# Reordering VectorE's first work in a routed-expert and gated-MLP kernel, and ending the block without GpSimd's drain

## The chip, the cores and the metric

The kernel runs on one core of a Trainium2 chip. Five engines work side by side, each with an instruction stream of its own: TensorE (PE in the views; its weight loads are PEld), VectorE (DVE), ScalarE (ACT), GpSimd (POOL) and SyncE (SP), which only starts transfers. They wait for each other through semaphores. The metric is device microseconds of one execution; fewer is better.

## What is computed

Tokens are normed, sent through one of four "experts" chosen by token id (all three products of an expert use the same 512x512 matrix from `ctx_2048`), added back under a gate, normed again and sent through a gated MLP of inner width 1408:

```python
def _L0_xattn_ref(hidden_states, token_ids, Wg, Wu, Wd):
    expert_ids = jnp.minimum(jnp.clip(token_ids, 0, VOCAB - 1) // (VOCAB // 4), 3)
    for e in range(4):
        g = jax.nn.silu(jnp.einsum('bsd,fd->bsf', hidden_states, Wg[e]))
        u = jnp.einsum('bsd,fd->bsf', hidden_states, Wu[e])
        y = jnp.einsum('bsf,df->bsd', g * u, Wd[e])
        out = jnp.where((expert_ids == e)[..., None], y, out)
    return out

x = x + jnp.tanh(g_xattn[0]) * _L0_xattn_ref(_layernorm(x), ids, ctx, ctx, ctx)
x = x + jnp.tanh(g_ffn[0])   * _L0_ffn_ref(_layernorm(x), gate_w, up_w, down_w, gate_s, up_s, down_s)
# ffn: silu(x @ gate_w.T * gate_s) * (x @ up_w.T * up_s) @ down_w.T * down_s
```

There are 2048 tokens of width 512, all float32. This is a reading cut of the reference: clipping, reshapes and the excluded inputs are left out.

## The kernel before

**Stages.** First a routing stage sorts the 2048 tokens by expert into 19 tiles of 128 slots (16 tiles of tokens and up to 3 more, since every expert's tokens are padded to whole tiles). It is a chain of small VectorE operations and of matmuls with one-hot matrices. From it come: `gidx`, which rows of `x` GpSimd gathers for each tile (column 0 is made first, by a product of its own, so that tile 0 can be fetched early; columns 1 to 18 follow at L620); `sidx`, where GpSimd stores a finished tile; `tiles` and from it `packed`, which expert each tile has, which TensorE reads into registers (L996); and a second set of one-hots, `is_low`, `is_high` and `in_tile` (L636 to L642), for a product (L991) that gives `oidx`, the order in which results are written at the very end.

Then come 19 expert steps, one for each tile, then the MLP in four blocks of four tiles, each block with 11 chunks of the inner width. The last four tiles' results are scaled, added and stored one by one.

**Products in two parts.** Every float32 operand is held as a high part (rounded, ScalarE: `ctx_hi`, `x_hi`, `h_hi`) and a low part (the rest, VectorE: `ctx_lo`, `x_lo`, `h_lo`). An expert product (`expert_product`, L951) is 12 matmuls in three passes of four: high by high, low `x` by high weights, high `x` by low weights. Its third pass waits for the low parts of the expert's matrix, `ctx_lo` of 4 chunks each, 16 chunks for the four experts (`ctx_lo(n_from, n_to)`, L740).

**A tile's way.** GpSimd gathers its rows; VectorE takes `stats` (L648 to L653), GpSimd the inverse deviation (`inverse_std`, L375), VectorE applies it (`norm`, L659); TensorE transposes (`turn_x`, L948), ScalarE and VectorE split (`x_hi` L464, `x_lo` L686); TensorE makes the first product (L962), ScalarE the silu (L472), VectorE the product with it (`hidden`, L697); TensorE transposes that (`turn_h`, L977), it is split (`h_hi` L468, `h_lo` L701), and the second product's result is added by VectorE (`update`, L708) and stored by GpSimd (L369).

**Order.** Every engine's order is written out by hand. TensorE's in the expert stage is `first_product(k)`, `turn_x(k+1)`, `second_product(k-1)`, `turn_h(k)`. VectorE's `step(k)` holds its share of it, and the 16 `ctx_lo` chunks are laid between the first steps by hand (L747 to L768). ScalarE's first work is `ctx_hi(0)`, `ctx_hi(1)`, `x_hi(0)`, `ctx_hi(2)`, `silu(0)`, `x_hi(1)`, `ctx_hi(3)`, the gates' tanh, and then `h_hi(0)`. SyncE loads experts 0 and 1, then waits for tile 0's rows before it loads experts 2 and 3 (L247 to L249). GpSimd's order is gather 0, 1 and 2, then `inverse_std(0)` and `inverse_std(1)`, then gather 3.

While experts run, the MLP's weights `raw` (L262) are loaded in 16 pieces and split, and rows of the down weights are loaded once more as `checked` (L272) to see whether they have low bits at all (`check`, L719). They have two slots, `c % 2`.

## Time and profile before

| | |
|---|---|
| median of 3 runs | 405.64 us (405.2 to 405.85) |
| the profiled execution's own time | 406.21 us |
| its span, from the first instruction to the last | 404.4 us |
| PE busy | 375.8 us, 93% of the span |
| DVE busy | 239.6 us, 59% |
| ACT busy | 139.8 us, 35% |
| POOL busy | 91.3 us, 23% |

The profile describes one execution, so its times of instructions belong to the 406.21 us one. The 1.8 us between that and its span lie before the first or behind the last instruction. Busy shares are averages over stages that have different limits; the order of time within the first 46 us and the last 6 us is what matters here.

### The profile page before, as it was taken

The page shows a single profiled execution, that of the slowest core. Times are in us where ns is not written, and L with a number is a line of the kernel's source. Part 1 is how long each engine was busy: PE and PEld are TensorE (multiplying, and loading weights), DVE is VectorE, ACT ScalarE, POOL GpSimd, SP SyncE. Part 2 cuts the span into 40 slices and gives each one's busy share as a digit, 9 for nine tenths or more (in the row PEclk, how much of TensorE's full clock was granted, in tenths as well). Part 3 has the DMA queues.
Part 4 walks back from the last instruction along what each step waited for, and adds up shares of the span by engine and source line. Part 5 has one row for each costly group of instructions (what it writes and reads, how often), then busy time and mean ns, then how long its engine had stood idle before and what let it go on. Part 6 is the DMA issues. An engine that isn't in the chain of part 4 may idle for free.

```text
span 404.4 us, 6054 instructions
## 1 busy us (share of the span) xinstructions
PE 375.8 (93%) x1775; PEld 307.6 (76%) x1775; DVE 239.6 (59%) x457; ACT 139.8 (35%) x241; POOL 91.3 (23%) x132
## 2 busy tenths in 40 slices
PE   3299999999999879999999999999999999999991
PEld 2267788888888667788888888888888888888880
DVE  6879878888888875635537225636325646322244
ACT  3264454555454334623232222322222231222220
POOL 6335545454542121001102101101201001200003
PEclk9999999999999999999999999999999999999996
DMA  6757444455625324420000220000220000100002
GB/s 208 258 162 220 134 140 149 142 173 181 210 84 158 122 74 150 118 105 0 0 2 26 79 104 0 0 0 26 78 104 0 0 0 26 76 2 0 0 2 106
DMA packets 14959, 34.55 MB, mean 85 GB/s; under 512 B 2401, under 2 KB 2401, under 8 KB 14945
## 3 DMA queue, kind: packets, MB, share of 16 engines
q1 hardware_dynamic: 10624, 20.21, 15.7%
q0 software_dynamic: 4320, 14.16, 10.2%
q8 instruction: 8, 0.13, 0.1%
q14 instruction: 7, 0.05, 0.0%
HBM read 25.19 MB, written 9.18 MB: 85 GB/s over the span
## 4 chain that ended last, share of the span: by engine, by line
PE 83%; DVE 7%; DMA 3%; issue 2%; POOL 2%; ACT 1%; POOLq 0%; DVEq 0%; SPq 0%; ACTq 0%
PE bank L1059 37%; PE bank L962 22%; PE bank L1066 18%; PE bank L948 4%; DMA rows<-dwT 2%; PE bank L977 2%; DVE work L744 1%; DMA x_rows<-rows,sidx 1%; POOL minus_j L346 1%; DVE xn L659 1%; DVE work L701 1%; DVE work L686 0%; DVE rows L708 0%; ACT work L460 0%; DVE rows L860 0%
## 5 line engine op out<-in xcount | busy, mean ns | idle before, releaser
L1059 PE MATMUL bank<-work,wgu 128*128 (+1 forms) x720 | 167.3, 385 | 1.5 <-DVE work L686 1.3
L1059 PEld LDWEIGHTS bank<-work,wgu 128*128 128x128 f32 x720 | 133.0, 188 | 29.2 <-issue 1.6
L962 PE MATMUL bank<-work 128*128 (+1 forms) x432 | 111.4, 407 | 1.6 <-ACT work L464 0.7
L962 PEld LDWEIGHTS bank<-work 128*128 128x128 f32 x432 | 80.1, 192 | 19.1 <-issue 1.9
L1066 PE MATMUL bank<-work,hp 128*128 128x512 f32 x352 | 88.5, 394 | 0.5 <-DVE hp L831 0.5
L826 DVE SCALAR_TENSOR_TENSOR sh<-bank,gs,sh 128x512 f32<-128x512 f32 (+1 forms) x45 | 33.2, 738 | 88.1 <-PE bank L1059 88.0
L1066 PEld LDWEIGHTS bank<-work,hp 128*128 128x128 f32 x352 | 65.1, 188 | 13.9 <-DVE hp L831 0.9
L521 ACT ACTIVATE sh<-bank,gs 128x512 f32<-128x512 f32 (+1 forms) x45 | 30.5, 678 | 86.3 <-PE bank L1059 85.5
L525 ACT ACTIVATE hp<-sh 128x512 fp32r<-128x512 f32 (+1 forms) x45 | 28.0, 622 | 84.5 <-DVE sh L826 84.5
L375 POOL TENSOR_TENSOR rstd<-ve,half 128x1 f32<-128x1 f32 x31 | 19.7, 635 | 131.4 <-DVE ve L653 131.2
L831 DVE TENSOR_TENSOR hp<-sh,hp 128x512 fp32r<-128x512 f32 (+1 forms) x45 | 30.6, 681 | 30.2 <-ACT hp L525 30.0
L447 POOL DMA_INDIRECT out<-rows,oidx x16 | 16.1, 1008 | 116.9 <-DVE rows L860 94.2
L686 DVE TENSOR_TENSOR work<-bank,work 128x512 fp32r<-128x512 f32 (+1 forms) x35 | 23.9, 684 | 1.5 <-ACT work L464 0.9
L464 ACT ACTIVATE work<-bank 128x512 fp32r<-128x512 f32 (+1 forms) x35 | 20.5, 590 | 12.4 <-PE bank L948 8.6
L948 PE MATMUL bank<-ident,xn 128*128 128x128 f32 x124 | 19.6, 283 | 4.5 <-DVE xn L659 4.5
L948 PEld LDWEIGHTS bank<-ident,xn 128*128 128x128 f32 x124 | 15.6, 145 | 9.6 <-DVE xn L659 6.1
L659 DVE TENSOR_SCALAR xn<-rows,mv,rstd 128x512 f32 (+1 forms) x31 | 17.0, 550 | 9.0 <-POOL rstd L375 9.0
L472 ACT ACTIVATE sh<-bank 128x512 f32<-128x512 f32 x19 | 11.4, 598 | 28.5 <-PE bank L962 28.4
L648 DVE BATCH_NORM_STATS2 bn<-rows 128x6 f32 (+1 forms) x31 | 21.2, 684 | 0.0
L708 DVE SCALAR_TENSOR_TENSOR rows<-bank,tg,rows 128x512 f32 (+1 forms) x19 | 14.2, 749 | 7.3 <-PE bank L962 7.3
L715 DVE TENSOR_TENSOR wgu<-raw,wgu (+1 forms) x16 | 14.3, 892 | 6.3 <-issue 6.3
L482 ACT ACTIVATE junk<-wgu 128x704 f32 x16 | 12.7, 794 | 13.2 <-DVE wgu L715 13.2
(126 smaller groups left out, 235.6 us busy)
## 6 DMA issues: line engine op xcount, KB each, us to landing
raw<-guT SPq DMA_DIRECT2D x16, 352.0 KB
ctx_in<-ctxT SPq DMA_DIRECT2D x4, 1024.0 KB, 7.9
rows<-x_rows SPq DMA_DIRECT2D x8, 512.0 KB, 4.1
checked<-dwT SPq DMA_DIRECT2D x11, 256.0 KB, 3.4
rows<-dwT SPq DMA_DIRECT2D x11, 256.0 KB, 3.0
dsb<-down_s SPq DMA_DIRECT2D x1, 256.0 KB, 8.1
out<-rows,oidx POOLq DMA_INDIRECT x16, 2.7
rows<-x,inow POOLq DMA_INDIRECT x12, 4.0
```

The lines of the kernel that those rows point to most:

```text
L464: act.activation(xpart(b, u, 0), turned[:, :], ACT.Copy).then_inc(S["xhi_ready"], 1)
L521: act.activation(sh[:, part], gate_ps(i)[:, part], ACT.Silu, scale=gs[:, 0, c:c + 1])\
L525: act.activation(hslot(c)[:, 0, part], sh[:, part], ACT.Copy)\
L648: dve.bn_stats(bn[:, 0, :], rows[:, ds(at, 1), :]).then_inc(S["bn_parts"], 1)
L659: dve.tensor_scalar(xn[:, :], rows[:, ds(at, 1), :], mv[:, 0, 0:1], rstd[:, 0:1], ALU.subtract, ALU.mult).then_inc(S["xn_ready"], 1)
L686: dve.tensor_tensor(xpart(b, u, 1), turned[:, :], xpart(b, u, 0).bitcast(F32), ALU.subtract)\
L826: dve.scalar_tensor_tensor(out=sh[:, part], in0=up_ps(i)[:, part], scalar=gs[:, 1, c:c + 1], in1=sh[:, part], op0=ALU.mult, op1=ALU.mult). ...
L831: dve.tensor_tensor(hslot(c)[:, 1, part], sh[:, part], hslot(c)[:, 0, part].bitcast(F32), ALU.subtract)\
L948: mm = pe.transpose(xt_ps[:, c * P:(c + 1) * P], xn[:, c * P:(c + 1) * P], ident[:, :])
L962: mm = pe.matmul(out_ps[:, :], part(s)[:, c * P:(c + 1) * P], ctx_w(e, c, w), start=n == 0, stop=n == last)
L1059: mm = pe.matmul(out_ps[:, tiles.start * P:tiles.stop * P], wgu[:, row + h, w, c * P:(c + 1) * P], moving, start=n == 0, stop=n == last)
L1066: mm = pe.matmul(acc_ps[u][:, :], hslot(c)[:, s, u * P:(u + 1) * P], down_w(c, w), start=c == 0 and n == 0, stop=c == IC - 1 and n == len( ...
```

## The change

VectorE's first work is put in another order. The arithmetic of the second one-hots moves ahead of the copy of `gidx` as far as its small operands go, and the one-hots come right behind that copy. The tables for storing (`sidx`) and for TensorE's registers (`packed`) become a function, `index_tables`, that is called after `norm(0)`. `stats(0)` comes before every `ctx_lo`; all later groups of `ctx_lo` hold one chunk fewer at each point, so that the last group, `ctx_lo(12, 16)`, has four chunks instead of three. TensorE reads its registers from `packed` behind `turn_x(1)` instead of ahead of `turn_x(0)`. SyncE loads a `checked` row when the row two before it is done (it has two slots), instead of the row one before. And the block ends without GpSimd's drain; in its place is nothing, and the other four engines' drain and report become two instructions each.

```diff
--- before.py
+++ after.py
@@ -237,7 +237,7 @@
 
             eng.sem_inc(S["held"])
 
-        block = ctx.enter_context(nc.Block())
+        block = ctx.enter_context(nc.Block(no_gpsimd_drain=True))
 
         @block.sync
         def _(sp):
@@ -291,7 +291,7 @@
                 next_piece(q)
                 before_q = CHECK_AT + RAWS - 2
                 c, c_before, c_checked = (sp.snap(q - before_q), sp.snap(16 * (q - before_q)),
-                                          sp.snap(q - before_q))
+                                          sp.snap(q - before_q - 1))
                 sp.wait_ge(S["check_landed"], c_before)
                 hold(sp)
                 sp.wait_ge(S["bits_done"], c_checked)
@@ -299,7 +299,7 @@
                 check_row(c)
             for c in range(2 + PIECES - checks_from, IC):
                 sp.wait_ge(S["check_landed"], 16 * c)
-                sp.wait_ge(S["bits_done"], c)
+                sp.wait_ge(S["bits_done"], c - 1)
                 check_row(c)
             def load_rows(b):
                 for half_, landed in enumerate((S["rows_a"], S["rows_b"])):
@@ -615,33 +615,36 @@
             dve.scalar_tensor_tensor(out=owner[:, 2, :], in0=tile_at[:, :], scalar=pad_end[0:1, 2:3],
                                      in1=owner[:, 1, :], op0=ALU.is_ge, op1=ALU.add)
             then(dve.tensor_scalar(owner[:, 3, :], tile_at[:, :], pad_end[0:1, 3:4], None, ALU.is_ge))
+            def over_out(a):
+                return a[:, :].unsqueeze(1).to_broadcast([P, TILES, CT])
+
+            then(dve.tensor_scalar(tile_up[:, :], rank[:, :], -(P - 1) / 2, ROUND, ALU.add, ALU.add))
+            dve.scalar_tensor_tensor(out=minus_low[:, :], in0=tile_up[:, :], scalar=ROUND,
+                                     in1=rank[:, :], op0=ALU.subtract, op1=ALU.subtract)
+            then(dve.tensor_scalar(high[:, :], tile_up[:, :], -ROUND, None, ALU.add))
             of_slot = bank[5][:, 0:2 * STEPS]
             dve.wait_ge(S["route_pe"], 4)
             dve.tensor_copy(gidx[:, 1:STEPS], of_slot[:, 1:STEPS]).then_inc(S["tables_ready"], 1)
-            dve.tensor_copy(tiles[:, :, :], owner[:, 2:4, :])
-            then(dve.scalar_tensor_tensor(out=empty[:, :], in0=of_slot[:, STEPS:], scalar=0.0,
-                                          in1=dump[:, :], op0=ALU.is_equal, op1=ALU.mult))
-            for i in range(2):
-                dve.tensor_tensor(shifted[:, i, :], tiles[:, 0, 1 - i:1 - i + PACKED], shifts[:, :],
-                                  ALU.logical_shift_left)
-            dve.scalar_tensor_tensor(out=sidx[:, :], in0=empty[:, :], scalar=-1.0, in1=of_slot[:, STEPS:],
-                                     op0=ALU.add, op1=ALU.add).then_inc(S["tables_ready"], 1)
-            then(dve.tensor_scalar(tile_up[:, :], rank[:, :], -(P - 1) / 2, ROUND, ALU.add, ALU.add))
-            dve.tensor_reduce(packed[:, :], shifted[:, :, :], AX, ALU.bitwise_xor)\
-               .then_inc(S["tables_ready"], 1)
-
-            then(dve.scalar_tensor_tensor(out=minus_low[:, :], in0=tile_up[:, :], scalar=ROUND,
-                                          in1=rank[:, :], op0=ALU.subtract, op1=ALU.subtract))
-            dve.tensor_scalar(high[:, :], tile_up[:, :], -ROUND, None, ALU.add)
+            is_out = is_high[:, 0:TILES, :]
             dve.tensor_tensor(is_low[:, :, :], minus_low[:, :].unsqueeze(1).to_broadcast([P, P, CT]),
                               minus_j[:, :, :], ALU.is_equal).then_inc(S["low_ready"], 1)
-            dve.wait_ge(S["low_ready"], 3)
-            is_out = is_high[:, 0:TILES, :]
-            then(dve.tensor_tensor(is_out, high[:, :].unsqueeze(1).to_broadcast([P, TILES, CT]),
-                                   tile_of[:, 0:TILES, :], ALU.is_equal))
-            dve.tensor_tensor(in_tile[:, 0, 0:TILES, :], is_out,
-                              token[:, :].unsqueeze(1).to_broadcast([P, TILES, CT]), ALU.mult)\
+            then(dve.tensor_tensor(is_out, over_out(high), tile_of[:, 0:TILES, :], ALU.is_equal))
+            dve.tensor_copy(tiles[:, :, :], owner[:, 2:4, :])
+            dve.tensor_tensor(in_tile[:, 0, 0:TILES, :], is_out, over_out(token), ALU.mult)\
                .then_inc(S["route_sb"], 1)
+
+            def index_tables():
+                dve.wait_ge(S["route_sb"], 4)
+                for i in range(2):
+                    dve.tensor_tensor(shifted[:, i, :], tiles[:, 0, 1 - i:1 - i + PACKED], shifts[:, :],
+                                      ALU.logical_shift_left)
+                then(dve.scalar_tensor_tensor(out=empty[:, :], in0=of_slot[:, STEPS:], scalar=0.0,
+                                              in1=dump[:, :], op0=ALU.is_equal, op1=ALU.mult))
+                dve.scalar_tensor_tensor(out=sidx[:, :], in0=empty[:, :], scalar=-1.0,
+                                         in1=of_slot[:, STEPS:], op0=ALU.add, op1=ALU.add)\
+                   .then_inc(S["tables_ready"], 1)
+                dve.tensor_reduce(packed[:, :], shifted[:, :, :], AX, ALU.bitwise_xor)\
+                   .then_inc(S["tables_ready"], 1)
 
             def stats(m, at):
 
@@ -744,28 +747,29 @@
                     dve.tensor_tensor(ctx_w(e, c, 1), ctx_in[:, e, c, :], ctx_w(e, c, 0).bitcast(F32),
                                       ALU.subtract).then_inc(S["ctx_lo"], 1)
 
-            ctx_lo(0, 3)
             landed(0)
             stats(0, ring_slot(0))
+            ctx_lo(0, 1)
+            norm(0, ring_slot(0))
+            index_tables()
+            ctx_lo(1, 3)
+            x_lo(0, 0, 0)
             ctx_lo(3, 4)
-            norm(0, ring_slot(0))
-            ctx_lo(4, 6)
-            x_lo(0, 0, 0)
             landed(1)
             stats(1, ring_slot(1))
-            ctx_lo(6, 7)
+            ctx_lo(4, 5)
             norm(1, ring_slot(1))
-            ctx_lo(7, 9)
+            ctx_lo(5, 8)
             hidden(0)
             x_lo(1, 0, 0)
             landed(2)
             stats(2, ring_slot(2))
-            ctx_lo(9, 10)
+            ctx_lo(8, 9)
             dve.wait_ge(S["gates_ready"], 1)
             step(1)
-            ctx_lo(10, 13)
+            ctx_lo(9, 12)
             step(2)
-            ctx_lo(13, 16)
+            ctx_lo(12, 16)
             with dve.Fori(3, CHECK_AT) as k:
                 step(k)
             dve.wait_ge(S["bits_clear"], 1)
@@ -991,13 +995,13 @@
                 mm = pe.matmul(bank[4][:, 0:TILES], is_low[:, :, c], in_tile[:, 0, 0:TILES, c],
                                start=c == 0, stop=c == CT - 1)
             mm.then_inc(S["route_pe"], 1)
-            pe.wait_ge(S["tables_ready"], 3)
-
-            these, ones_before = [pe.value_load(packed[0:1, i:i + 1], min_val=0, max_val=4 ** PACKED - 1)
-                                  for i in range(2)]
             turn_x(0)
             first_product(0, 0, ctx_ready=KC)
             turn_x(1)
+            pe.wait_ge(S["tables_ready"], 3)
+
+            these, ones_before = [pe.value_load(packed[0:1, i:i + 1], min_val=0, max_val=4 ** PACKED - 1)
+                                  for i in range(2)]
             turn_h(0)
 
             def expert_step(k, e=None, e_before=None, ctx_ready=None):
```

VectorE (DVE), from behind the copy of `gidx` (L620) to the statistics of tile 0, before. `is_low`, `is_high` and `in_tile` are the second one-hots, `empty`, `sidx`, `shifted` and `packed` the tables, `work<-ctx_in` is `ctx_lo`, BN_STATS opens `stats(0)`, `xn` is `norm(0)`:

```order
L622 SCALAR_TENSOR_TENSOR empty<-bank,dump 128x19
L625 TENSOR_TENSOR shifted<-tiles,shifts 1x15 x2
L627 SCALAR_TENSOR_TENSOR sidx<-empty,bank 128x19
L629 TENSOR_SCALAR tile_up<-rank 128x16
L630 TENSOR_REDUCE packed<-shifted 1x2
L633 SCALAR_TENSOR_TENSOR minus_low<-tile_up,rank 128x16
L635 TENSOR_SCALAR high<-tile_up 128x16
L636 TENSOR_TENSOR is_low<-minus_low,minus_j 128x2048
L640 TENSOR_TENSOR is_high<-high,tile_of 128x256
L642 TENSOR_TENSOR in_tile<-is_high,token 128x256
L744 TENSOR_TENSOR work<-ctx_in,work 128x512 x3
L648 BN_STATS bn<-rows 128x6
```

The same engine from behind the same copy (now L627), in the changed kernel:

```order
L629 TENSOR_TENSOR is_low<-minus_low,minus_j 128x2048
L631 TENSOR_TENSOR is_high<-high,tile_of 128x256
L632 CAST tiles<-owner 1x38
L633 TENSOR_TENSOR in_tile<-is_high,token 128x256
L651 BN_STATS bn<-rows 128x6
L654 BN_AGGR mv<-bn 128x2
L656 TENSOR_SCALAR ve<-mv 128x1
L747 TENSOR_TENSOR work<-ctx_in,work 128x512
L662 TENSOR_SCALAR xn<-rows,mv,rstd 128x512
L639 TENSOR_TENSOR shifted<-tiles,shifts 1x15 x2
L641 SCALAR_TENSOR_TENSOR empty<-bank,dump 128x19
L643 SCALAR_TENSOR_TENSOR sidx<-empty,bank 128x19
```

The table rows moved from ahead of the one-hots to behind `xn`; three `work<-ctx_in` no longer stand ahead of BN_STATS; `tile_up`, `minus_low` and `high` moved to before the copy of `gidx`, above the first row shown.

VectorE again, from the MLP piece of step 2 to the loop over the later tiles, before; `wgu` is the piece's low part, `sh` is `hidden(2)`, `rows` is `update(1)`, and `work<-ctx_in` is `ctx_lo` once more:

```order
L715 TENSOR_TENSOR wgu<-raw,wgu 128x704
L697 TENSOR_TENSOR sh<-bank,sh 128x512
L686 TENSOR_TENSOR work<-bank,work 128x512
L708 SCALAR_TENSOR_TENSOR rows<-bank,tg,rows 128x512
L744 TENSOR_TENSOR work<-ctx_in,work 128x512 x3
L769 UNCONDITIONAL_BRANCH
L701 TENSOR_TENSOR work<-bank,work 128x512
```

And in the changed kernel:

```order
L718 TENSOR_TENSOR wgu<-raw,wgu 128x704
L700 TENSOR_TENSOR sh<-bank,sh 128x512
L689 TENSOR_TENSOR work<-bank,work 128x512
L711 SCALAR_TENSOR_TENSOR rows<-bank,tg,rows 128x512
L747 TENSOR_TENSOR work<-ctx_in,work 128x512 x4
L773 UNCONDITIONAL_BRANCH
L704 TENSOR_TENSOR work<-bank,work 128x512
```

One more chunk stands between the update of tile 1 and the low part of tile 2's hidden values, which opens the loop (L701).

TensorE (PE) around the registers, before, from the last products of the routing to the first turn of hidden values (L977):

```order
L929 MATMUL bank<-in_tile,is_low 128x38 x16
L991 MATMUL bank<-in_tile,is_low 128x16 x16
L996 TENSOR_LOAD packed
L996 ISA x2
L996 TENSOR_LOAD packed
L996 ISA x2
L948 MATMUL bank<-ident,xn 128x128 x4
L962 MATMUL bank<-work 128x512 x12
L948 MATMUL bank<-ident,xn 128x128 x4
L977 MATMUL bank<-ident,sh 128x128 x4
```

And in the changed kernel:

```order
L933 MATMUL bank<-in_tile,is_low 128x38 x16
L995 MATMUL bank<-in_tile,is_low 128x16 x16
L952 MATMUL bank<-ident,xn 128x128 x4
L966 MATMUL bank<-work 128x512 x12
L952 MATMUL bank<-ident,xn 128x128 x4
L1003 TENSOR_LOAD packed
L1003 ISA x2
L1003 TENSOR_LOAD packed
L1003 ISA x2
L981 MATMUL bank<-ident,sh 128x128 x4
```

The two loads, with two register instructions each, moved past the first turn, the first product and the second turn.

## Rows read from the trace of the kernel before

**Rows 1.** The page: its span, and the chain that ended last, by engine.

```profile
span 404.4 us, 6054 instructions
...
PE 83%; DVE 7%; DMA 3%; issue 2%; POOL 2%; ACT 1%; POOLq 0%; DVEq 0%; SPq 0%; ACTq 0%
```

**Rows 2.** Windows: stretch, its us, busy us of each engine, PEclk, DMA share, GB/s.

```profile
19.77:25.26 5.49, 5.49 (x13) 4.23 (x14) 4.01 (x8) 2.19 (x4) 1.93 (x2) 1.00 0.68 225
...
45.66:126.17 80.51, 80.51 (x401) 66.29 (x400) 66.60 (x124) 40.53 (x76) 40.04 (x59) 1.00 0.48 150
...
163.75:392.25 228.50, 227.99 (x1043) 189.15 (x1043) 103.47 (x176) 63.42 (x102) 18.93 (x24) 1.00 0.09 31
```

**Rows 3.** Timeline, end of routing: start us, us, engine, line, what [idle before <-releaser].

```profile
9.40 0.22 DVE L617 TENSOR_SCALAR owner<-tile_at,pad_end 1x19 f32<-1x19 f32 x1
...
10.25 0.18 DVE L620 CAST gidx<-bank 128x18 uint32<-128x18 f32 x1 [0.64 <-PE bank L929]
...
10.71 0.94 POOL L364 DMA_INDIRECT rows<-x,gidx  x1 [0.37 <-DVE gidx L620]
...
11.48 1.22 DVE L636 TENSOR_TENSOR is_low<-minus_low,minus_j 128x2048 f16<-128x2048 f16 x1
11.96 1.56 POOL L364 DMA_INDIRECT rows<-x,gidx  x1 [0.30 <-issue]
...
12.81 0.99 SPq L249 DMA_DIRECT2D ctx_in<-ctxT  x2
13.06 0.29 DVE L642 TENSOR_TENSOR in_tile<-is_high,token 128x256 f16<-128x256 f16 x1
13.27 1.89 DVE L744 TENSOR_TENSOR work<-ctx_in,work 128x512 fp32r<-128x512 f32 x3
```

**Rows 4.** Timeline, tile 0's way to the first product, and expert 2's arrival.

```profile
15.08 0.69 DVE L648 BATCH_NORM_STATS2 bn<-rows 128x6 f32<-128x512 f32 x1
...
16.37 0.96 POOL L375 TENSOR_TENSOR rstd<-ve,half 128x1 f32<-128x1 f32 x1 [2.85 <-DVE ve L653]
...
17.37 0.55 DVE L659 TENSOR_SCALAR xn<-rows,mv,rstd 128x512 f32<-128x512 f32 x1 [0.48 <-POOL rstd L375]
...
17.97 1.12 PE L948 MATMUL bank<-ident,xn 128*128 128x128 f32 x4 [3.32 <-DVE xn L659]
...
19.77 5.49 PE L962 MATMUL bank<-work 128*128 128x512 f32 x12 [0.69 <-ACT work L464]
...
20.44 2.19 ACT L460 ACTIVATE work<-ctx_in 128x512 fp32r<-128x512 f32 x4 [0.72 <-DMA ctx_in<-ctxT]
...
25.93 0.69 DVE L697 TENSOR_TENSOR sh<-bank,sh 128x512 f32<-128x512 f32 x1 [1.51 <-ACT sh L472]
...
26.58 2.18 ACT L460 ACTIVATE work<-ctx_in 128x512 fp32r<-128x512 f32 x4
```

**Rows 5.** Line L249, the loads of experts 2 and 3: time from issue to landing.

```profile
DMA to landing us min/median/max: 7.6/8.7/9.8
```

**Rows 6.** Timeline, the last groups of low parts and the products waiting for them.

```profile
34.78 1.89 DVE L744 TENSOR_TENSOR work<-ctx_in,work 128x512 fp32r<-128x512 f32 x3
...
36.20 0.76 PEld L962 LDWEIGHTS bank<-work 128*128 128x128 f32 x4 [0.27 <-issue]
...
37.78 0.66 PE L948 MATMUL bank<-ident,xn 128*128 128x128 f32 x4 [0.38 <-DVE xn L659]
```

**Rows 7.** Timeline, the same for the product of tile 3.

```profile
42.00 1.89 DVE L744 TENSOR_TENSOR work<-ctx_in,work 128x512 fp32r<-128x512 f32 x3
...
44.03 1.17 PE L962 MATMUL bank<-work 128*128 x4 [0.44 <-DVE work L744]
```

**Rows 8.** Line L996: engine, op, count, duration ns min/median/max, first and last start.

```profile
L996 PEldq TENSOR_LOAD <-packed x2: 314/407/500, 13.6 to 14.4; - x2
```

**Rows 9.** Line L76, the barrier at the block's end, columns as above.

```profile
L76 POOLq DRAIN  x1: 5687/5687/5687, 398.5 to 398.5; - x1
...
L76 SPq DRAIN  x1: 7/7/7, 401.7 to 401.7; - x1
```

6 lines of the change are left out of this document (3 added, 3 removed).

## The prediction

> **What bounds the kernel now.** I first read the page's chain by engine and the windows by stage [rows 1, 2]. The reader is to see that PE holds 83% of the chain, and that it is busy for all of the 80.51 us of the steady expert steps and 227.99 of 228.50 us of the MLP. Nothing that VectorE, SyncE or GpSimd do sooner in those stages shows in the end time; they just begin sooner or later as a whole. Time can be won ahead of 45.66 us, where PE still waits, and behind 392 us, where it is done.
>
> Then the timeline of the start [rows 3, 4]. The first product starts at 19.77 at the end of one chain: `in_tile` 13.06, three `ctx_lo` 13.27, statistics 15.08, GpSimd's power 16.37, `xn` 17.37, turn 17.97, `x_hi`, product. PE sat idle 3.32 us for `xn`. But tile 0's rows had landed by 12.81: SyncE starts the loads of experts 2 and 3 when it sees them, and that row starts there. So the statistics stood 2.27 us behind their data, held up by one-hots and weights on their own engine.
>
> Last, the barrier [rows 9]. SyncE, which has seen all results land, drains at 401.7 in 7 ns. GpSimd's drain starts at 398.46 and takes 5.687 us, to 404.15. The span ends at 404.4, so the last 2.4 us are GpSimd's drain alone, although the chain of the page gives it less.
>
> **The change, part by part.**
>
> *Second one-hots sooner.* `tile_up`, `minus_low` and `high` go into the 0.64 us in which VectorE idles ahead of the `gidx` copy at 10.25 [rows 3]. From the last `owner` (9.40, 0.22 long) a dependent step each 0.26 us (estimate from the spacing there) puts the copy at 10.27: no loss. `is_low` then starts at about 10.37 instead of 11.48. From its start to that of `in_tile` were 1.58 us and 0.29 of `in_tile`, so these end by 12.24, ahead of the landing at 12.8. The statistics then start at 12.84 instead of 15.08: **2.24 us sooner**, bound now by the gather.
>
> *Down to the first product.* Same instructions behind it: power, `xn`, turn, `x_hi`. One `ctx_lo` lies between statistics and `xn` as before, under the 0.96 us power. `xn` starts at 15.13, the turn at 15.73, the product at 17.53.
>
> *Does the power find GpSimd free?* It would start at 14.13. GpSimd ahead of it issues gathers 1 and 2: 0.94 us from 10.71, and 1.56 us from 11.96 to 13.52, the long one while `is_low` ran (11.48 to 12.70) [rows 3]. In the new order `is_low` (10.37 to 11.6) lies over gather 1 instead. If the two only swap lengths, GpSimd is free at 13.5 or so: cost 0. If both take 1.56 with the gap of 0.30, it is free at 14.15: cost about 0.05. I take 0. The Trainium skill, "SBUF — State Buffer", section "SBUF: two separate sides" (the trap box), says that GpSimd cannot write descriptors at all while VectorE holds the shared port pair. By that, gather 1 waits for `is_low` until 11.6, then takes 0.94, and gather 2 ends between 13.8 and 14.4: cost 0 to 0.3, and the sum would be 402.0 instead of 401.7. The row agrees in sign (1.56 against 0.94), not with a full block.
>
> *Tables and weights behind.* `index_tables` is at most the 1.2 us between 10.25 and 11.48, less the copy and `tile_up`: I take 0.7. From the end of `xn` at 15.6: tables to 16.3, two `ctx_lo` (0.63 each from 1.89 for three) to 17.5, `x_lo` 17.5 to 18.2. The second pass of the first product needs `x_lo` four matmuls in, at 17.53 + 4 x 0.457 = 19.4 [rows 2]: covered, with 1.2 us to spare. The third needs chunk 3 at 21.2; it is there at 18.9. Statistics and `xn` of tile 1 end at 21.6, three more chunks at 23.4; `hidden(0)` is due at 25.93 - 2.24 = 23.69 [rows 4]. It fits with 0.3 to spare.
>
> *Does ScalarE follow?* Expert 2's data lands at 20.44 regardless, and its four copies end at 22.6, ahead of `silu(0)` at 23.1. Expert 3's: second issue at 13.2 plus at most 9.8 is 23.0 [rows 5], and its copies would start at 26.58 - 2.24 = 24.3 [rows 4]. Both free by the time that they are needed, so `h_hi(0)` and what follows it go 2.24 us sooner.
>
> *Registers on TensorE.* Two loads, 0.50 and 0.31 us, began at 13.6 [rows 8], 0.25 us after `in_tile` (13.06 + 0.29), for which the 16 matmuls ahead of them wait [rows 3]: the sequencer had run ahead of the array. Behind `turn_x(1)` they should lie under the first product of 5.49 us. Bounds: 0, and 1.5 us (13.6 to 15.1) if they wait for the turn to finish. Even then `turn_h(0)` moves from 24.4 to 25.4, and its reader `h_hi(0)` waits for expert 3's copies until 26.5. I take 0.
>
> *One chunk fewer ahead.* Step 2's product needs 12 chunks for its third pass. Before, that was the second of the group at 34.78; its loads began at 36.20. Now it is the third: 0.6 later, so the product ends 0.6 later. PE then stood idle 0.38 us for `xn`, and a matmul's 0.2 more lies in its end, so about **0.06** reaches the turn [rows 6]. Step 3 needs 16 chunks, now the fourth of its group instead of the third: the four matmuls at 44.03 waited for just that (0.44 us) [rows 7], and the low part of tile 2's hidden values stands behind it too. This is **0.6** in full. Nothing covers it; the new wait is here.
>
> *What of the start reaches the steady state:* 2.24 - 0.06 - 0.6 = 1.6; I take **1.5**, for slack of a tenth that hand reckoning misses. It is kept to the end, since PE is never idle afterwards.
>
> *SyncE's check rows* go up to one step sooner, right behind the MLP piece. They share the DMA engines with gathers, at a mean share of 0.48 [rows 2]. Their readers are on VectorE, and PE's 80.51 of 80.51 us cover them. 0, both ways; without that cover, a gather late by half a load would cost a microsecond or so in one step.
>
> *No drain.* SyncE reports at 401.71 instead of GpSimd at 404.15. The release behind that took 0.2 us to the span's end. With one more instruction per engine, the span would end at 402.0: **2.4 us**. Bounds: 2.4, and 0 if the work that it waits for must be done after the last instruction anyway.
>
> **Sum.** The profiled execution is 406.21 (span 404.4 and 1.8 around it): 406.2 - 1.5 - 2.4 = 402.3. It was 0.57 above the median. By the median, 405.64 - 3.9 = **401.7 us**, 1.0% less.
>
> **The rivals.** A measurement of this kernel tells about 0.2%, 0.8 us, from no change.
>
> *The drain comes back outside the span.* Profile: span about 400.5, but the execution 4.2 us longer than its span instead of 1.8. For it: a drain of 5.7 us waits for something real, since the last issue ended at 399.65. Against it: all results had landed by 401.5. Time 404.1.
>
> *The start gives nothing.* VectorE now waits bare for tile 0's rows; with 0.3 us to spare at `hidden(0)` and a gather or the power late, the ramp may fall back to its old limit, the four chunks at step 3. Against it: each covered step above has its row. Time 403.2 with the drain gained, about 405.6 without.
>
> *Slower: TensorE's clock.* In the stretch of the first product PEclk reads 1.00, but 12 matmuls took 5.49 us, 457 ns each, against 227.99 / 1043 = 219 ns in the MLP [rows 2]: the lower level, 1.2 of 2.4 GHz. Before it PE had idled 3.32 us. A product at that level costs 2.86 us more. If the new order leaves more of the ramp at it, time is lost: 3.9 + 0.8 is passed from the second extra product that nothing covers, which gives 401.7 + 5.7 = 407.4. Against it: PE does the same work in the same order, closer together. If the rise comes at the same absolute time as before (behind the 5.49 us stretch), the turn and two or three matmuls are slow, 0.2 each, and the wait for `xn` hides them. The Trainium skill, "TensorE: Matmul & The Clock Gate", section "What's actually happening", says that the point of the rise does not follow the kernel's start and varies from run to run. By that it may also come inside the first product, for at most 0.3 us of gain, since `hidden(0)` finds VectorE busy until 23.4; no row here shows it.
>
> **How the numbers follow.** Main case 0.60 (its own range 400.9 to 402.6: 0.3 of clock and 0.5 of noise below, 0.3 of gathers and register loads and 0.6 of noise above). Drain back, start gained 0.17 (404.1). Drain gone, start not 0.12 (403.2). Neither 0.07 (405.6). Slower 0.04 (407.4). Faster by over 0.2%: 0.60 + 0.17 + 0.12 = 0.89. Same 0.07, slower 0.04. The range from 400.8 to 404.3 takes in the first three and leaves 0.11 and the tails out.
>
> **What the profile would show.** Right: BN_STATS of tile 0 at about 12.9, the first product at 17.5, four chunks in a row ahead of step 3's last pass, steady steps from about 44.1; no GpSimd drain in the barrier, the span's end 0.3 us behind SyncE's drain, at about 400.5. Wrong: the power behind a gather still being issued; PE idle ahead of `turn_h(0)` with register loads in the gap; a first product after the first at 457 ns a matmul; a time further from the span than 1.8 us; or a first gather that lands later than 12.8.

## The result and the profile after

| | before | after |
|---|---|---|
| median, us | 405.67 (405.2 to 405.85, 4 runs) | 401.39 (401.28 to 402.06, 4 runs) |
| ratio | | 0.9905, 95% interval 0.9889 to 0.9922 |
| profiled execution, us | 406.21 | 402.06 |
| its span, us | 404.4 | 400.3 |

Forecast were 401.7 us and a range of 400.8 to 404.3. On another chip the changed kernel took 401.29 (ratio 0.9895). The profiled execution of the changed kernel is the longest of its four, 0.7 us above their median, and that of the kernel before is 0.5 above its own.

The timeline of the changed kernel's start, to be read against [rows 3, 4] (start us, us, engine, line, what, idle before and what ended it):

```profile
10.21 0.18 DVE L627 CAST gidx<-bank 128x18 uint32<-128x18 f32 x1
10.30 1.22 DVE L629 TENSOR_TENSOR is_low<-minus_low,minus_j 128x2048 f16<-128x2048 f16 x1
10.66 1.68 POOL L364 DMA_INDIRECT rows<-x,gidx  x1 [0.46 <-DVE gidx L627]
...
12.64 0.69 DVE L651 BATCH_NORM_STATS2 bn<-rows 128x6 f32<-128x512 f32 x1 [0.52 <-DMA rows<-x,gidx]
12.64 0.95 POOL L364 DMA_INDIRECT rows<-x,gidx  x1 [0.30 <-issue]
...
13.77 0.68 DVE L747 TENSOR_TENSOR work<-ctx_in,work 128x512 fp32r<-128x512 f32 x1
13.94 0.96 POOL L375 TENSOR_TENSOR rstd<-ve,half 128x1 f32<-128x1 f32 x1 [0.35 <-issue]
14.93 0.55 DVE L662 TENSOR_SCALAR xn<-rows,mv,rstd 128x512 f32<-128x512 f32 x1 [0.48 <-POOL rstd L375]
...
15.53 1.12 PE L952 MATMUL bank<-ident,xn 128*128 128x128 f32 x4 [2.12 <-DVE xn L662]
...
17.34 5.19 PE L966 MATMUL bank<-work 128*128 128x512 f32 x12 [0.69 <-ACT work L464]
...
21.54 1.88 DVE L747 TENSOR_TENSOR work<-ctx_in,work 128x512 fp32r<-128x512 f32 x3
...
23.35 0.68 DVE L700 TENSOR_TENSOR sh<-bank,sh 128x512 f32<-128x512 f32 x1
...
24.08 0.66 PE L981 MATMUL bank<-ident,sh 128*128 128x128 f32 x4 [1.12 <-DVE sh L700]
```

The statistics now wait, with nothing left in front of them, for the gather (0.52 us, released by the DMA) and start at 12.64 instead of 15.08, 2.44 sooner. The two gathers have swapped lengths: the one under `is_low` takes 1.68, the one behind it 0.95 (before: 0.94 and 1.56), and the power does not wait for them. Everything down to the product keeps its spacing: 17.34 against 19.77. `hidden(0)` (L700) has no idle time of its own in front: VectorE comes to it straight from the three chunks at 21.54.

The next piece of the same timeline is where the low parts bound the ramp, to be read against [rows 6, 7]:

```profile
31.75 1.89 DVE L747 TENSOR_TENSOR work<-ctx_in,work 128x512 fp32r<-128x512 f32 x3
33.78 1.17 PE L966 MATMUL bank<-work 128*128 x4 [0.45 <-DVE work L747]
...
38.98 2.49 DVE L747 TENSOR_TENSOR work<-ctx_in,work 128x512 fp32r<-128x512 f32 x4
41.61 1.19 PE L966 MATMUL bank<-work 128*128 x4 [1.05 <-DVE work L747]
...
43.19 2.98 PE L966 MATMUL bank<-work 128*128 x12
```

The last row is the product that stood at 45.41 before. PE's wait at step 3 has grown from 0.44 to 1.05 us: the fourth chunk. The lead over before, 3.0 us at the updates of tiles 0 and 1 (L711, 31.08 and 38.31 against 34.12 and 41.34), is 2.4 at the four waiting matmuls and 2.2 in the last row.

The barrier of the changed kernel (engine, op, count, duration ns, first and last start), against [rows 9]:

```profile
L76 POOLq EVENT_SEMAPHORE  x2: 17/17/17, 399.9 to 400.0; - x2
...
L76 SPq DRAIN  x1: 7/7/7, 399.8 to 399.8; - x1
```

No row of a GpSimd drain is left. The span ends 0.5 us behind SyncE's drain instead of 2.7 behind it, and the execution is 402.06 - 400.3 = 1.8 us longer than its span, as before.

### The profile page after: what moved, and what is told of

Read it like the earlier page. It is cut to its first block, busy times and chain, and to the rows that moved or that the text cites. A ratio compares the mean times of both kernels' runs of the same rounds, so it can differ in the third digit from the quotient of the medians.

```text
span 400.3 us, 6063 instructions
## 1 busy us (share of the span) xinstructions
PE 375.2 (94%) x1775; PEld 307.2 (77%) x1775; DVE 239.7 (60%) x457; ACT 139.8 (35%) x241; POOL 92.6 (23%) x132
## 4 chain that ended last, share of the span: by engine, by line
PE 83%; DVE 8%; DMA 4%; issue 2%; POOL 2%; ACT 1%; DVEq 0%; SPq 0%; POOLq 0%
PE bank L1063 37%; PE bank L966 22%; PE bank L1070 18%; PE bank L952 4%; DMA x_rows<-rows,sidx 2%; DVE work L747 2%; PE bank L981 2%; DMA rows<-dwT 1%; DVE work L689 1%; POOL rows L364 1%; DVE xn L662 1%; POOL rstd L375 0%; DMA ids_i<-ids 0%; DVE rows L711 0%; DVE rows L864 0%
## 5 line engine op out<-in xcount | busy, mean ns | idle before, releaser
L521 ACT ACTIVATE sh<-bank,gs 128x512 f32<-128x512 f32 (+1 forms) x45 | 30.5, 678 | 86.3 <-PE bank L1063 85.6
L711 DVE SCALAR_TENSOR_TENSOR rows<-bank,tg,rows 128x512 f32 (+1 forms) x19 | 14.2, 750 | 7.3 <-PE bank L966 7.3
```

The source lines that it names most:

```text
L521: act.activation(sh[:, part], gate_ps(i)[:, part], ACT.Silu, scale=gs[:, 0, c:c + 1])\
```

## The experiments

Each was timed against the kernel before on the same chip, in three sets: the medians of before were 405.41 (9 runs), 405.35 (23) and 405.60 (14 runs, besides one of 645.4 that is left out; with it 405.68). The ratios are worked out from the single runs and differ a little from those of the medians. "Steady" is below the start of the product that stands at 43.19 in the changed kernel's profile.

### One half at a time: the drain back, and the drain alone

```diff
-        block = ctx.enter_context(nc.Block(no_gpsimd_drain=True))
+        block = ctx.enter_context(nc.Block())
```

> The changed kernel, only with GpSimd's drain back at the block's end. Theory (the two gains add, and the drain is worth what its record shows): about 403.7 us, 2.2 to 2.4 over the changed kernel's 401.4, with a GpSimd drain record that ends some 2.3 us behind SyncE's. Rival (the drain's work must be done after the last instruction anyway): 401.4, with the time between span and execution shorter by 2 us than without the drain.

The new order with the old end took **404.09 us** (403.45 to 404.34), ratio 0.9964 (0.9949 to 0.9978). So the order, with the register loads and the check rows that go with it, gives 1.3 us by the medians, 1.5 by the ratio.

The kernel before with the opposite edit:

> The kernel before, only without GpSimd's drain. Theory (additive): 405.67 - 2.2 = 403.5 us. Rival: 405.7, the drain's time comes back outside the span. Together with the run that puts the drain back, it says what the reordering alone gives: theory 1.9 to 2.0 us.

It took **402.93 us** (402.26 to 403.57), ratio 0.9939 (0.9924 to 0.9954): the drain alone gives 2.5 us. The two ratios multiply to 0.9903; both edits together measured 0.9905. They add, and nothing comes back outside the span: 402.26 - 400.3 = 1.96 us around it here, 404.09 - 402.1 = 1.99 with the drain in.

The barrier of the new order with the drain:

```profile
L76 POOLq DRAIN  x1: 5688/5688/5688, 396.2 to 396.2; - x1
...
L76 SPq DRAIN  x1: 7/7/7, 399.5 to 399.5; - x1
```

The drain is as long as before (5.69 us) and again the last to report, at 401.9 against SyncE's 399.5. It starts 2.3 us sooner than in [rows 9], and SyncE's drain comes 2.2 sooner: what it costs is how far it reaches past SyncE's drain, which waits for the last results to land, 2.4 us in both.

The profile of the drain alone holds a second lesson. Its order is that of before, but its steady product starts at 43.72, not 45.41. The place where it parts from [rows 4] is the first product:

```profile
19.54 4.40 PE L962 MATMUL bank<-work 128*128 128x512 f32 x12 [0.69 <-ACT work L464]
...
24.61 0.69 DVE L697 TENSOR_TENSOR sh<-bank,sh 128x512 f32<-128x512 f32 x1 [0.43 <-ACT sh L472]
```

Same instructions, 4.40 us instead of 5.49. TensorE began the product at its lower level (1.2 GHz, 457 ns a matmul in [rows 2, 4]) and rose to the higher one (2.4 GHz) within it, where in the profile of before that came only behind it. PEclk reads 1.00 over the whole product in both profiles, so it does not show this; the lengths do. The weight loads of the product, first before and then with the drain alone (duration ns min/median/max, first and last start):

```profile
L962 PEld LDWEIGHTS bank<-work x12: 287/330/334, 19.8 to 24.2; 128*128 128x128 f32 x12
```

```profile
L962 PEld LDWEIGHTS bank<-work x12: 187/328/333, 19.5 to 23.3; 128*128 128x128 f32 x12
```

A load takes 188 ns (median) in the steady steps of the changed kernel; only the second profile reaches that within the product, and its next turn takes 0.60 us where that of before took 1.00. So a part of the 2.2 us by which the profiles of before and of the changed kernel differ at the steady steps is this, and not the edit: with before's order they differ by 1.7 us between themselves (45.41 and 43.72).

### The statistics late, the registers early

The changed kernel with the `ctx_lo` groups of before:

```diff
+            ctx_lo(0, 3)
             landed(0)
             stats(0, ring_slot(0))
-            ctx_lo(0, 1)
+            ctx_lo(3, 4)
             norm(0, ring_slot(0))
             index_tables()
-            ctx_lo(1, 3)
+            ctx_lo(4, 6)
...
-            ctx_lo(12, 16)
+            ctx_lo(13, 16)
```

> The changed kernel with the groups of low parts laid as in the kernel before: three chunks ahead of tile 0's statistics, three in the last group. Theory (statistics at their data are worth what they come sooner, less the fourth chunk at step 3): statistics 1.3 later, the last group 0.6 shorter, so 0.5 to 0.7 over the changed kernel's 401.4: 402.0 us. Rival (VectorE's total of work sets the ramp, and its order does not matter): 401.4, or 400.9 for the shorter last group.

It took **402.17 us** (401.54 to 402.62), ratio 0.991 (0.9889 to 0.9931). In its profile the statistics start at 13.79 instead of 12.64, the first product at 18.47 instead of 17.34, but the steady product only 0.26 later (43.45): with one chunk fewer at the end, PE's wait at step 3 is 0.44 again. Of 1.15 us at the start, a quarter reaches the steady steps. The time, 0.8 above the changed kernel's on other chips, agrees in sign; its interval holds no difference too. Set beside the drain alone (0.9939), the run is also the nearest to the other half of the order: one-hots, tables and register loads moved, the chunks left where they were, 0.991. That would be 1.2 of the 1.5 us, but the two intervals touch, and no run moved the one-hots alone.

The register loads put back ahead of `turn_x(0)`, where `packed` now comes late:

```diff
+            pe.wait_ge(S["tables_ready"], 3)
+
+            these, ones_before = [pe.value_load(packed[0:1, i:i + 1], min_val=0, max_val=4 ** PACKED - 1)
+                                  for i in range(2)]
             turn_x(0)
             first_product(0, 0, ctx_ready=KC)
             turn_x(1)
-            pe.wait_ge(S["tables_ready"], 3)
-
-            these, ones_before = [pe.value_load(packed[0:1, i:i + 1], min_val=0, max_val=4 ** PACKED - 1)
-                                  for i in range(2)]
```

> The changed kernel with TensorE's two register loads put back ahead of turn_x(0), while the tables stay behind norm(0). Theory (the moved loads are what lets the turn go at once): the turn waits for packed at 16.0 and then for the loads, 1.5 us, so it starts near 17.6 instead of 15.5; the ramp loses most of that: 403.2 us (402.7 to 403.6). Rival (the loads cost nothing wherever they stand, since VectorE sets the ramp): 401.4 to 401.9.

It took **403.43 us** (403.15 to 404.31), ratio 0.9947 (0.9932 to 0.9962), 2.0 us more than the changed kernel. The row that shows it:

```profile
17.57 1.11 PE L952 MATMUL bank<-ident,xn 128*128 128x128 f32 x4 [4.21 <-issue]
```

`xn` was there at 15.4, `packed` at 16.0, the loads lay from there to 17.3 (L1000), and PE turned at 17.57, with "issue" for a releaser. So the move of the loads is not an ornament of the change: without it, tables behind `norm(0)` give back more than the new order wins. In the changed kernel the loads start at 21.7 and 22.6 (312 and 502 ns), under the end of the first product and the turn behind it, while PE still waits for `sh`.

### SyncE's check rows one step sooner

The waits of before (`c_checked` and `c` instead of one less) in the changed kernel:

```diff
-                                          sp.snap(q - before_q - 1))
+                                          sp.snap(q - before_q))
...
-                sp.wait_ge(S["bits_done"], c - 1)
+                sp.wait_ge(S["bits_done"], c)
```

> The changed kernel, with SyncE's check rows waiting for the row one before again. Theory (TensorE covers whatever these rows do in the steady steps): 401.4 us, the same within 0.3 as the changed kernel on this chip, and the steady steps' products at the same times within 0.1 us. Rival (the earlier check rows crowd the DMA engines at the change to the MLP, where TensorE waits for rows and down weights): 0.5 to 1 us faster than the changed kernel, and the MLP starts sooner by that.

**401.59 us** (400.84 to 401.68), ratio 0.9896; the changed kernel beside it on the same chip 401.29 (400.96 to 401.83), ratio 0.9895:

> The changed kernel once more, beside the three below on one chip. Theory (the change is worth 1.5 us of start and 2.5 us of drain): 401.4 us, ratio 0.990. Rival (part of the first measurement was chance): 402 us or more.

This part of the change costs and brings nothing that can be measured: the five runs of each average 401.42 and 401.37 us. The rival, earlier check rows that crowd the change of stage and cost 0.5 to 1 us, is not borne out; a difference below about half a microsecond would not show.

### Is TensorE's clock to be had sooner?

Nine matmuls of 512 columns whose result nobody reads, in TensorE's idle times ahead of the first product. They add work and change no output:

```diff
+            warm(4)
             pe.wait_ge(S["low_ready"], 3)
...
             mm.then_inc(S["route_pe"], 1)
+            warm(4)
             turn_x(0)
+            warm(1)
             first_product(0, 0, ctx_ready=KC)
```

> The changed kernel with nine matmuls of 512 columns of no use in TensorE's idle time ahead of the first product (four before the oidx product, four behind it, one behind the first turn), so that the clock has risen when it starts. Theory (at this order VectorE is busy until 23.4 and holds the hidden values of tile 0, so the clock is worth little more): the first product takes about 3 us instead of 5.2, steady steps 0 to 0.4 sooner, 401.1 us. Rival (TensorE's level sets the ramp): the whole 2.3 us reach the end, 399.3 us.

> The kernel before (with the drain and the old order) with the same nine matmuls. Theory (part of what the reordering seemed to give is that the clock rises inside or ahead of the first product instead of behind it): the hidden values of tile 0 go 1.5 sooner, 404.1 us, and against the warmed changed kernel only 0.5 to 1 us is left beside the drain. Rival (the clock has no part in it): 405.4, and the reordering is worth its full 1.5 us between the two warmed kernels.

In the changed kernel: **400.79 us** (400.47 to 402.64), ratio 0.9887 (0.9862 to 0.9911). In the kernel before: **404.87 us** (403.92 to 405.9), ratio 0.9983 (0.9967 to 0.9999). The first products:

```profile
17.32 5.20 PE L971 MATMUL bank<-work 128*128 128x512 f32 x12 [0.26 <-ACT work L464]
```

```profile
19.84 5.09 PE L967 MATMUL bank<-work 128*128 128x512 f32 x12 [0.26 <-ACT work L464]
```

PE's idle time ahead is filled (0.26 instead of 0.69 us), and the product is still slow: 5.20 us, like the 5.19 without them. So these two runs test little: what both expected hangs on a product much shorter than it was. The times leave it open too. In the changed kernel no gain stands clear of the intervals. In the kernel before, the added matmuls gain 0.7 us by the ratio, with an interval that all but reaches 1, and why is not shown.

The trace of each profile also records from when the higher level was granted. Over all profiles taken here:

| order | start of the first product, its length, higher level from, us (one profile each) |
|---|---|
| before's | 19.77, 5.49, 25.86 |
| before's, drain alone left out | 19.54, 4.40, 22.54 |
| before's, with added matmuls | 19.84, 5.09, 24.30 |
| changed kernel | 17.34, 5.19, 22.04 |
| changed kernel, repeated | 17.31, 4.38, 20.25 |
| new order, with added matmuls | 17.32, 5.20, 22.05 |
| new order, the six other variants with the start at 17.3 to 17.5 | lengths 4.68 to 5.49, level from 20.92 to 23.34 |
| new order, statistics late | 18.47, 5.07, 22.90 |
| new order, registers early | 19.37, 5.49, 25.52 |

The sooner behind its start the level rises, the shorter the product; when the rise comes 5.6 us or more behind the start, it is 5.49. The moment changes from execution to execution of the same kernel (22.04 and 20.25 are both the changed kernel), and in the one profile with added matmuls it is 22.05. What decides the moment is open.

The table goes some way to explain why the reorder is worth more in some executions than in others. With before's order `hidden(0)` follows the product: 25.93 after 5.49 us, 24.61 after 4.40. With the new order it does not, up to a length of 5.33 us: 23.35 after 5.19, and in the execution with 4.38:

```profile
17.31 4.38 PE L966 MATMUL bank<-work 128*128 128x512 f32 x12 [0.69 <-ACT work L464]
...
23.31 0.68 DVE L700 TENSOR_TENSOR sh<-bank,sh 128x512 f32<-128x512 f32 x1
```

0.8 us of product are worth 0.04 there, since VectorE's own queue of chunks ends at 23.4. At the steady steps the same two profiles are 0.43 apart all the same (43.19 and 42.76), so the rest of the ramp varies too. The scatter of the times proves nothing either way: the runs of before have standard deviations of 0.41, 0.76 and 0.54 us in the three sets, the nine of the changed kernel on two chips 0.33, and its six with added matmuls 0.83.

### Chunks moved into VectorE's idle time

If the group of four at step 3 is what bounds the ramp, every chunk out of it is worth 0.6 us. First one chunk into the 0.52 us ahead of tile 0's rows:

```diff
+            ctx_lo(0, 1)
             landed(0)
             stats(0, ring_slot(0))
-            ctx_lo(0, 1)
+            ctx_lo(1, 2)
...
-            ctx_lo(12, 16)
+            ctx_lo(13, 16)
```

> The changed kernel with the first chunk of low parts (ctx_lo 0) moved ahead of the wait for tile 0's rows, where VectorE idles 0.52 us, and every later group shifted by one chunk, so that the last group has three chunks instead of four. Theory (the fourth chunk of the last group stands bare on the path at step 3, the gap is nearly free): tile 0's statistics 0.1 later, the steady steps 0.5 sooner, 400.9 us. Rival (the ramp's length is set elsewhere, by the transfers or TensorE): 401.4, or 401.5 for the late statistics.

**401.24 us** (400.88 to 402.23), ratio 0.9892 (0.9877 to 0.9908). The chunk ran from 12.02 to 12.69, the statistics started 0.04 later than in the changed kernel, and PE's wait at step 3 fell to 0.44:

```profile
40.94 1.18 PE L967 MATMUL bank<-work 128*128 x4 [0.44 <-DVE work L747]
...
42.52 2.98 PE L967 MATMUL bank<-work 128*128 x12
```

0.67 us sooner at the steady steps (43.19 to 42.52), as the chunk theory has it, with the first product at the same 5.19. But the time is the same within the measurement. Its profile is that of the longest of the four runs, 402.23 us, and loses the gain behind the last expert step, in the change to the MLP:

```profile
145.60 7.55 PE L1064 MATMUL bank<-work,wgu 128*128 x32 [1.34 <-DVE work L689]
...
155.63 3.93 PE L1064 MATMUL bank<-work,wgu 128*128 x16 [0.67 <-ACT sh L521]
...
162.03 3.94 PE L1064 MATMUL bank<-work,wgu 128*128 x16 [0.66 <-ACT sh L521]
```

Two waits of 0.67 and 0.66 us. The chain of the same execution says for what:

```profile
146.53 5.07 DMA x_rows<-rows,sidx
...
151.62 2.73 DMA rows<-dwT
...
156.22 4.53 DMA rows<-dwT
```

A store of finished rows and two loads of down weights, one after the other. ScalarE copies the down weights (L514) ahead of its next silu (L521), and PE waits for that silu; so the MLP's second and third chunk wait for the transfers, whatever PE brought along. The changed kernel has the same two waits, of 0.25 and 0.28 us; its repetition only the second, 0.30; eight of the fourteen profiles show none. Where the three other runs, 400.88 to 401.39 us, lose the 0.67 us, if they do, was not seen.

Then the idle time filled further: one more chunk out of the last group, which then has two, and the tables into VectorE's wait for the power (GpSimd's `inverse_std`):

```diff
+            ctx_lo(0, 1)
             landed(0)
             stats(0, ring_slot(0))
-            ctx_lo(0, 1)
-            norm(0, ring_slot(0))
+            ctx_lo(1, 2)
             index_tables()
-            ctx_lo(1, 3)
+            norm(0, ring_slot(0))
+            ctx_lo(2, 4)
...
             stats(1, ring_slot(1))
-            ctx_lo(4, 5)
+            ctx_lo(5, 7)
             norm(1, ring_slot(1))
-            ctx_lo(5, 8)
+            ctx_lo(7, 10)
...
-            ctx_lo(12, 16)
+            ctx_lo(14, 16)
```

> The changed kernel with one chunk of the low parts ahead of tile 0's rows, the tables in VectorE's wait for the deviation of tile 0, two chunks ahead of the norm of tile 1, and so a last group of two chunks instead of four. Theory (each chunk out of the last groups is worth 0.6 us at step 3): steady steps 1.2 to 1.3 us sooner than the changed kernel's, time 400.2 if the change to the MLP gives that on, 400.7 if it takes half of it. Rival (with three chunks the ramp has already reached its other limits, tile 2's and 3's own chains): the same as with one chunk ahead of the rows alone, 401.2 us.

**400.63 us** (399.99 to 400.72), ratio 0.9872 (0.9853 to 0.9891), 0.7 us less than the changed kernel on the same chip, whose lowest run is 400.96. The intervals of the two ratios overlap, but all four runs lie below all five of the changed kernel. The profile:

```profile
39.00 3.13 PE L967 MATMUL bank<-work 128*128 x12
...
42.33 3.00 PE L967 MATMUL bank<-work 128*128 x12
...
39.51 1.28 DVE L747 TENSOR_TENSOR work<-ctx_in,work 128x512 fp32r<-128x512 f32 x2
```

Step 3's product, the first row, is one row of 12 again; PE waits for no chunk. The steady steps are only 0.86 sooner than in the changed kernel's profile and 0.43 than in that of its repetition (42.76), not 1.2 to 1.3. The expectation had left out that once the chunks no longer bind, the first product's length does. It was 5.49 here, its silu starts on ScalarE at 23.03 and takes 0.60, and `hidden(0)` stands at 23.70, behind it. The MLP's first chunks show no wait in this profile, so its 0.7 us reach the end.

### Chunks moved to GpSimd

Chunks 12 to 15 made by GpSimd between its gathers, VectorE's last group gone (the calls and TensorE's wait are left out of this cut):

```diff
+            def pool_lo(n):
+                e, c = n // KC, n % KC
+                pool.wait_ge(S["ctx_hi"], n + 1)
+                pool.tensor_tensor(ctx_w(e, c, 1), ctx_in[:, e, c, :], ctx_w(e, c, 0).bitcast(F32),
+                                   ALU.subtract).then_inc(S["ctx_pool"], 1)
...
             step(2)
-            ctx_lo(12, 16)
```

> The changed kernel with the last four chunks of low parts (expert 3's) made by GpSimd in its gaps between gathers instead of by VectorE, so that VectorE's last group falls away. Theory (that group stands bare on the path at step 3 and TensorE becomes the limit behind it): the second product of tile 2 starts 1.2 sooner, 400.2 us. Rival (GpSimd's subtraction is slow or slows VectorE beside it, and delays gathers): 401.4 or more.

**403.55 us** (402.32 to 405.85), ratio 0.996 (0.9937 to 0.9982), 2 us worse. The place:

```profile
31.60 4.64 DVE L757 TENSOR_TENSOR work<-ctx_in,work 128x512 fp32r<-128x512 f32 x3
33.19 2.49 POOL L387 TENSOR_TENSOR work<-ctx_in,work 128x512 fp32r<-128x512 f32 x2
36.38 1.18 PE L977 MATMUL bank<-work 128*128 x4 [3.19 <-DVE work L757]
```

GpSimd's two chunks lie over VectorE's three, and those take 4.64 us instead of 1.89: 2.75 more, about the 2.49 that GpSimd worked. One chunk alone has all of it, and the others took what they always take (duration ns min/median/max):

```profile
L757 DVE TENSOR_TENSOR work<-ctx_in,work x3: 681/687/3436, 31.6 to 32.8; 128x512 fp32r<-128x512 f32 x3
```

The Trainium skill ("SBUF — State Buffer", section "SBUF: two separate sides") says that the two engines share a port pair which one of them holds at a time, for a VectorE operation with two SBUF inputs; by that, this overlap must serialize, and the trace agrees. Single chunks of GpSimd beside operations that read PSUM took 1.28 us, and VectorE's operations kept their lengths.

So two chunks were left to GpSimd, where it had done no harm, on top of the filled idle time:

> The kernel of the idle time filled, with chunks 12 and 13 on GpSimd besides, placed in its gaps at about 23.7 and 29.7 us, where a chunk did no harm when four were moved there. VectorE's group after step 2 is then gone. Theory (GpSimd takes a chunk in 1.3 us and costs only where VectorE reads two SBUF operands at the same time): steady steps 1.5 to 2.2 us sooner than the changed kernel's, time about 399.8 us. Rival (VectorE's chunks and GpSimd's lie over each other again, as the group of three that took 4.64 instead of 1.89 us): 401 us or more, with a group of low parts on VectorE at over 1 us a chunk in the timeline.

The median of its ten runs is **400.27 us**, but seven took 399.83 to 400.53 and the other three 405.57 to 407.57; ratio 0.9886 (0.9854 to 0.9918), worked out without the two longest. The profile is of one of the seven: steady product 41.91, 1.3 us sooner than the changed kernel's instead of the 1.5 to 2.2 expected, with a first product of 5.49 us once more, and GpSimd's chunks clear of VectorE's but for 0.1 us.

```profile
24.62 1.28 POOL L387 TENSOR_TENSOR work<-ctx_in,work 128x512 fp32r<-128x512 f32 x1 [2.31 <-ACT work L468]
...
30.25 1.28 POOL L387 TENSOR_TENSOR work<-ctx_in,work 128x512 fp32r<-128x512 f32 x1
```

What the three long runs do differently is not known, as none was profiled. The kernel with four chunks on GpSimd is split too (six runs of 402.3 to 403.0, six of 404.1 to 405.9). The version with all chunks on VectorE is the one to keep: 400.63, lowest of the kernels whose runs agree.

## Why the prediction was right

- **The drain** (2.4 us): measured alone 2.5 (0.9939). The rival by which it returns outside the span is refuted by that, and by 1.8 us around the span of before and of the changed kernel alike.
- **Statistics 2.24 us sooner**: 2.44 in the profile, of which 0.18 is the gather's earlier landing in that execution. That the gather, not VectorE, would bound it was right.
- **GpSimd's gathers cost nothing for the power**: right in size; swapped lengths, 1.68 and 0.95, GpSimd free at 13.59 and the power's input ready at 13.85. But "not with a full block" misread the row. A gather's issue under a two-operand operation of VectorE ended 0.82 to 0.83 us behind that operation three times: before, `is_low` to 12.70 and the gather to 13.52; after, 11.52 and 12.34; with the statistics late, three chunks to 13.86 and the gather to 14.69:

```profile
11.98 1.88 DVE L747 TENSOR_TENSOR work<-ctx_in,work 128x512 fp32r<-128x512 f32 x3
...
12.58 2.11 POOL L364 DMA_INDIRECT rows<-x,gidx  x1 [0.30 <-issue]
```

  So all but some 0.1 of the 0.95 us waits until VectorE is through. By the rule that the prediction took from the Trainium skill ("SBUF — State Buffer", section "SBUF: two separate sides"), gather 1 would end 0.94 behind the end of `is_low`, at 12.46; it ended at 12.34. The trace agrees with the rule, and the cost was 0 because gather 2 met no such operation. Not every operation that follows holds a gather on: in the changed kernel the one at 39.83 began under the second of four chunks that start 0.6 us apart from 38.98, took 1.34 us and ended at 41.17, 0.9 behind the second, while the other two ran.
- **Registers hidden**: right (21.7 to 22.9, the turn at 24.08 right behind `sh`); the 2.0 us of the run with the loads ahead of the turn are the price without that place.
- **`hidden(0)` fits with 0.3 to spare**: it stands at 23.35, where VectorE's queue ends, and its silu was done at 23.16, since the level rose within the product. The spare time was gone before it was used: what the prediction had as a side remark, that a shorter product gains at most 0.3 us, holds. A product of up to 5.33 us no longer sets `hidden(0)`; one of 5.49 did, with the idle time filled (23.70).
- **One chunk fewer, 0.06 at step 2 and 0.6 at step 3**: right. PE waits 0.45 at step 2, and the lead over before goes from 3.04 us ahead of it to 2.99 behind it; at step 3 PE waits 1.05 instead of 0.44, and the lead goes from 3.02 to 2.42. One chunk taken back out gave 0.67 us.
- **1.5 us of start**: 1.3 to 1.5 measured with the drain back. By the two profiles alone it looks like 2.2 at the steady steps and 1.9 at SyncE's drain, in part because the profile of before had the slow first product. The sum also lacks a gain that these profiles show: `h_lo(0)` goes from 29.45 (L701), where it waited 0.32 us for ScalarE, to 26.41 (L704), 3.0 sooner, where `hidden(0)` is 2.6 sooner. That the total came out at 1.5 may owe something to this term and the next one standing against each other.
- **"Kept to the end, since PE is never idle afterwards"**: wrong. [rows 2] covers 45.66 to 126.17 and 163.75 to 392.25, and the stretch between them was never read. There PE can wait for stores and down weights, and of the profiles' 2.45 us at the MLP's first product (148.64 to 146.19) 1.9 is left at the third chunk's (163.75 to 161.84). The chunk in the gap lost all of its 0.67 us there in its profile. For this change the loss was within the bounds; half a microsecond more can be lost there whole. What makes that stretch of transfers end at a different time in each execution stays open; by the medians the check rows are not it.
- **The slower rival, the clock**: it did not come. The product took 5.19 us, not longer than before, and no later product ran at 457 ns a matmul.

## What to carry to other kernels

Look at what the last engine in the closing barrier does there: a drain that ends behind the results' landing is bare time, here 2.5 of 4.3 us for one argument. What the drain guards in other kernels no run here shows. Work taken off the critical chain's first stretch has to go somewhere; count it where it piles up (a fourth chunk was 0.6 us), and fill the idle times ahead of a landing and during a wait for another engine first (another 0.7 us), but keep VectorE's long two-operand operations off GpSimd's short ones that the chain waits for (0.96 instead of 0.57 us). One profile of each kernel can differ by a microsecond in a start that no edit touched, so run each half of a change alone, look where the profiled execution stands among the runs, and read every stretch up to the end before a gain is called kept.

## What the hardware showed beyond that

The same first product took 4.38 to 5.49 us over the fourteen profiles, shorter the sooner TensorE's higher level came within it; in the one profile of the changed kernel with nine added matmuls ahead of it, it was not shorter (5.20 us).

A two-operand operation of GpSimd over one of VectorE cost VectorE about GpSimd's whole length (4.64 instead of 1.89 us beside 2.49). A gather's issue that begins under a long one of VectorE's is held too (1.68 us under `is_low`, 2.11 under three chunks, 0.95 alone).

The same holds for the power, and it is on tile 0's way before and after the change alike. All powers of the changed kernel (duration ns min/median/max):

```profile
L375 POOL TENSOR_TENSOR rstd<-ve,half x31: 545/572/1135, 13.9 to 321.5; 128x1 f32<-128x1 f32 x31
```

The one of tile 0 takes 0.96 us, under the `ctx_lo` chunk that runs from 13.77 to 14.45, and ends 0.45 behind that chunk; those of tiles 1 and 2, each under a chunk, take 0.93 and 0.94, and the usual one 0.57. So the chunk laid "under" the power is not free. By these rows `norm(0)` could start some 0.4 us sooner without it (an estimate, 0.96 less 0.57); every kernel here, the one with the idle time filled too, keeps that chunk there, and no run has tried it.

How GpSimd's chunks can split a kernel's runs into two groups, over 5 us apart with two chunks (400.5 and 405.6) and from 403.0 to 404.1 with four, is not explained.
